# The second feed-forward stage with tokens sorted by expert into 63 tiles of 128 rows, in place of 40 dense blocks

## The reference

```python
def _L0_ffn_ref(hidden_states, gate_w, Wg, Wu, Wd, cWg, cWu, cWd):
    ...
        _, sel = jax.lax.top_k(scores, TOP_K)                 # 4 of 32
        w = jnp.take_along_axis(rw, sel, axis=-1)
        w = w / w.sum(axis=-1, keepdims=True)
    ...
    def _moe(x2d, Wg, Wu, Wd, cw):
        g = jnp.einsum('th,ehi->eti', x2d, Wg)
        u = jnp.einsum('th,ehi->eti', x2d, Wu)
        a = jax.nn.silu(g) * u * cw.T[:, :, None]
        return jnp.einsum('eti,eih->th', a, Wd)
    ...
    cw_large = jnp.zeros((T, NUM_EXPERTS), x.dtype).at[rows, sel].add(w)
    cw_small = jnp.zeros((T, NUM_CHUNK), x.dtype).at[rows, sel // GROUP].add(w)
    large = _moe(x, Wg, Wu, Wd, cw_large)
    small = _moe(x, cWg, cWu, cWd, cw_small)
    return (large + SMALL_SCALE * small).reshape(B, S, H)     # SMALL_SCALE = 0.05
```

## Time and profile before

| | before |
|---|---|
| median of 3 runs | 1463.18 us (1459.61 to 1463.65) |
| span of the profiled execution | 1454.0 us |
| median less that span | 9.2 us |
| mean granted TensorE clock | 0.802 |
| busy: PE, DVE, ACT, POOL | 86%, 78%, 55%, 38% of the span |
| first matmul of stage 1's loop, first write of stage 2's xn | 100.01 us, 430.30 us |

### The profile page before, as it was taken

The page is one execution under the profiler, slowest core; times in us unless marked ns, Lnnn a source line. Parts: engine busy times, 40 slices in busy tenths (PEclk is TensorE's granted clock), DMA queues, the critical chain, the costliest instruction groups (busy, mean ns, idle before and its releaser), DMA issues.

```text
span 1454.0 us, 30518 instructions
## 1 busy us (share of the span) xinstructions
PE 1257.3 (86%) x11458; PEld 770.0 (53%) x11458; DVE 1131.6 (78%) x2427; ACT 802.3 (55%) x1526; POOL 559.2 (38%) x619
## 2 busy tenths in 40 slices
PE   6878999999987999875899864888888989996998
PEld 3554565566553233234688742555555655563555
DVE  7858666666669999978788679898898767659785
ACT  4452444444436988873344345899899943334432
POOL 5450000000001005000333437899898938773362
PEclk9999999999996555557899985555555589997999
DMA  6111343343324999991578425998999811111010
GB/s 222 44 54 41 102 126 119 108 126 119 97 66 82 182 172 172 182 177 42 148 197 217 110 59 104 153 151 153 149 154 155 136 62 44 44 55 33 12 33 30
DMA packets 356784, 161.06 MB, mean 111 GB/s; under 512 B 330112, under 2 KB 332800, under 8 KB 356272
## 3 DMA queue, kind: packets, MB, share of 16 engines
q1 hardware_dynamic: 353344, 151.96, 48.8%
q0 software_dynamic: 1728, 4.72, 1.3%
q10 hardware_dynamic: 1584, 2.68, 0.6%
HBM read 76.79 MB, written 2.29 MB: 54 GB/s over the span
## 4 chain that ended last, share of the span: by engine, by line
PE 47%; DVE 29%; POOL 9%; ACT 5%; DMA 4%; issue 4%; SPq 1%; ACTq 0%; POOLq 0%; DVEq 0%
PE s_all L922 32%; DVE small L2397 8%; PE bank L922 6%; POOL c_hi L831 3%; POOL c_lo L831 2%; PE s_all L1331 2%; POOL c_hi L829 2%; PE s_all L1141 1%; DVE small L2400 1%; DVE stats L1909 1%; PE bank L1141 1%; DVE ffbuf L2239 1%; DVE xt_lo L1930 1%; DVE x L2255 1%; DVE xn L1922 1%
## 5 line engine op out<-in xcount | busy, mean ns | idle before, releaser
L922 PE MATMUL s_all<-xt_hi,w_hi 128*128 128x512 f16 x576 | 171.8, 380 | 17.2 <-DVE ffbuf L2195 6.6
L922 PE MATMUL s_all<-xt_hi,w_lo 128*128 128x512 f16 x576 | 171.8, 380 | 0.0
L922 PE MATMUL s_all<-xt_lo,w_hi 128*128 128x512 f16 x576 | 171.8, 380 | 0.0
L1742 ACT ACTIVATE ag<-s_all,small 128x1024 int16<-128x1024 f32 x128 | 154.1, 1204 | 23.8 <-DVE small L2400 13.8
L2397 DVE TENSOR_REDUCE small<-s_all 128x1 f32<-128x1024 f32 x128 | 155.5, 1215 | 7.8 <-PE s_all L1331 7.8
L1331 PE MATMUL s_all<-ag 32*128 32x512 f16 x256 | 130.6, 612 | 13.3 <-ACT ag L1742 8.4
L745 POOL CAST ag<-region 128x512 f16<-128x512 f32 x4 | 2.4, 611 | 346.4 <-DVE region L2361 346.4
L1582 ACT ACTIVATE hid_hi<-ffbuf 128x512 f16<-128x512 f32 x80 | 50.4, 630 | 141.1 <-DVE ffbuf L2195 141.1
L1396 PE MATMUL s_all<-ag 32*128 32x256 f16 x512 | 91.0, 399 | 35.0 <-DVE small L2477 31.4
L1804 ACT ACTIVATE ag<-ffbuf,small 128x256 f32<-128x256 f32 x256 | 115.8, 507 | 0.2
L675 POOL TENSOR_TENSOR w_hi<-w_in,ws_col 128x768 f16<-128x768 f32 (+1 forms) x40 | 56.3, 1408 | 142.5 <-PE bank L922 126.4
(11 more groups left out here) (399 smaller groups left out, 3426.7 us busy)
## 6 DMA issues: line engine op xcount, KB each, us to landing
w_in<-in_w_blocks SPq DMA_DIRECT2D x76, 384.0 KB, 4.1
w_in<-in_w_experts SPq DMA_DIRECT2D x48, 320.0 KB, 4.6
sel<-token_weights SPq DMA_DIRECT2D x46, 256.0 KB, 3.8
sel<-token_weights SPq DMA_DIRECT2D x13, 384.0 KB, 3.5
region<-in_w_attn SPq DMA_DIRECT2D x4, 512.0 KB, 10.5
sel<-token_weights SPq DMA_DIRECT2D x13, 128.0 KB, 3.9
ag<-ag SPq DMA_TRANSPOSE x66, 3.4
x<-in_x_in SPq DMA_DIRECT2D x2, 512.0 KB, 4.7
```

The lines of the kernel that those rows point to most:

```text
L922: m = nc.tensor.matmul(outp, lhs, rhs, start=(first and n == 0), stop=(last and n == len(steps) - 1), skip_group_check=True)
L1742: nc.scalar.activation(p2[n % P2_BUFS], s2[n % S2_BUFS], ACT.Exp, bias=small[:, 1, s * L2_UNITS + v:s * L2_UNITS + v + 1], scale=scale_g[s ...
```

## The change

Stage 1 no longer multiplies every token by every expert. The 4096 picks (1024 tokens by 4) are ranked by expert, and each expert's picks are rounded up to whole tiles of 128 rows; there are always 63 tiles, which is enough for any choice of the tokens. Steps, by engine:

- SP loads the weights in 16 pairs of 1 MB (two large experts and their small one); three of these loads now stand ahead of the loads of stage 0's blocks 4 to 7, and behind those blocks comes one DMA that fills the 8.3 MB of `slots1` with zeros. POOL splits three pairs into high and low parts (`pairs1`, in the manner of L675 to L679), ACT and DVE the other 13 (39 units). All stay in SBUF (`arena`).
- DVE and PE compute each pick's place (`idx1`) and a table of two offsets per tile, which say where in `arena` the weights of its experts begin.
- POOL scatters the rows of xn (high and low part, 1 KB) to their places in DRAM, in 32 indirect DMAs (L817). When all have landed, SP reads one tile after another back in transposed form (L708, five buffers).
- PE runs 63 tiles: it loads the two offsets into registers, and issues 24 matmuls of 128 columns, whose weights stand at addresses computed from the registers, and 6 of 256 columns. ACT makes the silu and the high part, DVE product and low part, now on 128 x 256 numbers each, and copies the result out of PSUM; SP stores it to DRAM (`outs1`, L713).
- POOL then gathers the results of each token's picks in 32 indirect DMAs (L826), and DVE adds each, times its weight, to x. `context2` and six units of `context4` now run on PE and ACT behind the tiles.

```diff
-SELECTED = [1]
-SEL_BLOCKS = max(FFN[l][1] for l in SELECTED)
-SPREAD = SEL_BLOCKS - 4
-SPREAD_LANDED = 16 * 2 * (SPREAD // 2)
...
+TILES1 = T * TOP1 // P + E1 - 1
...
+SPLIT1_POOL = 3
+UNITS1 = 3 * (PAIRS1 - SPLIT1_POOL)
...
+XT1_BUFS = 5
+Z1_BUFS = 2 * TOP1
+Y1_BUFS = 4
...
-CTX_GAPS = {1: (0, 3), 2: (3, 6), 3: (7, 8)}
+CTX_GAPS = {3: (7, 8)}
...
+            def pair_load(c):
+                if c >= 4:
+                    sp.wait_ge(we_land[c % 4], 16 * (c // 4))
+                if c == 9:
+                    sp.wait_ge(s_setup, 1 + len(resident))
+                if c == 12:
+                    sp.wait_ge(w_split, FFN[0][1])
+                if c == 14:
+                    sp.wait_ge(blk_done, 2 * FFN[0][1])
+                sp.dma_start(staged1(c), w_pairs[c]).then_inc(we_land[c % 4], 16)
+
+            def tile_turn(n):
+                b = n % XT1_BUFS
+                if n >= XT1_BUFS:
+                    sp.wait_ge(ex_u, n - XT1_BUFS + 1)
+                sp.dma_start(xt1[b], slots1[n * P:(n + 1) * P, :], transpose=True).then_inc(land5[b], 16)
+
+            def tile_store(n):
+                b = n % Y1_BUFS
+                sp.wait_ge(ex_out, n + 1)
+                sp.dma_start(outs1[n * P:(n + 1) * P, :], y1[b]).then_inc(land4[b], 16)
...
+            for c in range(SPLIT1_POOL):
+                pair_load(c)
+            weight_blocks(1, 2)
+            sp.wait_ge(s_setup, 1)
+            sp.dma_start(slots1.rearrange("(p n) d -> p n d", p=P),
+                         zeros16[:, :].unsqueeze(1).broadcast_to([P, TILES1, 2 * D])).then_inc(s_table, 16)
+            for c in range(SPLIT1_POOL, PAIRS1):
+                pair_load(c)
+            sp.wait_ge(ex_rows, PUT1)
+            for n in range(XT1_BUFS):
+                tile_turn(n)
+            for n in range(TILES1):
+                if n + XT1_BUFS < TILES1:
+                    tile_turn(n + XT1_BUFS)
+                if n > 1:
+                    tile_store(n - 2)
+            for n in range(TILES1 - 2, TILES1):
+                tile_store(n)
...
+            def experts1():
+
+                pool.wait_ge(s_table, 16)
+                pool.wait_ge(ex_x, 1)
+                pool.wait_ge(e1_route, 3)
+                for i in range(NT):
+                    for j in range(TOP1):
+                        nc.gpsimd.indirect_dma_start(
+                            out=slots1, out_offset=bass.IndirectOffsetOnAxis(ap=idx1[:, i, j:j + 1], axis=0),
+                            in_=rows1[:, i, :], in_offset=None).then_inc(ex_rows, 16)
+                for b in range(Y1_BUFS):
+                    pool.wait_ge(land4[b], stored1(b))
+                for i in range(NT):
+                    if i > 1:
+                        pool.wait_ge(e1_add, TOP1 * (i - 1))
+                    for j in range(TOP1):
+                        nc.gpsimd.indirect_dma_start(
+                            out=z1[(i * TOP1 + j) % Z1_BUFS], out_offset=None, in_=outs1,
+                            in_offset=bass.IndirectOffsetOnAxis(ap=idx1[:, i, j:j + 1], axis=0)
+                        ).then_inc(e1_got[i % 2], 16)
...
+                pe.wait_ge(e1_route, 5)
+                pe.wait_ge(we_first, 12 * SPLIT1_POOL)
+                pe.wait_ge(we_lo, UNITS1)
+                pe.wait_ge(ex_rows, PUT1)
+                fill(10)
+
+                offs = {}
+
+                def gate_up(n):
+                    large = pe.value_load(table[0:1, 0, n:n + 1], min_val=0, max_val=(PAIRS1 - 1) * 2 * PW + 2 * LW)
+                    small_ = pe.value_load(table[0:1, 1, n:n + 1], min_val=0, max_val=(PAIRS1 - 1) * 2 * PW + 4 * LW)
+                    offs[n] = (large, small_)
+                    pe.wait_ge(land5[n % XT1_BUFS], 16 * (n // XT1_BUFS + 1))
+                    if n > 2:
+                        pe.wait_ge(ex_hid, n - 2)
+                    xt = xt1[n % XT1_BUFS]
+                    for a in range(2):
+                        for base, low, width, c in ((large, LW, INTER1, 0), (small_, SW, P, P)):
+                            outp = bank[n % 3][0:width, 2 * a * P + c:2 * a * P + c + P]
+                            for k in range(KT):
+                                o = (2 * k + a) * width
+                                hi, lo = [arena16[:, bass.ds(base + (o + q), width)] for q in (0, low)]
+                                nc.tensor.matmul(outp, hi, xt[:, k, :], start=(k == 0), stop=False, skip_group_check=True)
+                                nc.tensor.matmul(outp, hi, xt[:, KT + k, :], start=False, stop=False, skip_group_check=True)
+                                m = nc.tensor.matmul(outp, lo, xt[:, k, :], start=False, stop=(k == KT - 1),
+                                                     skip_group_check=True)
+                    m.then_inc(ex_u, 1)
+
+                def down(n):
+                    large, small_ = offs.pop(n)
+                    pe.wait_ge(ex_hl, n + 1)
+                    if n > 3:
+                        pe.wait_ge(ex_out, n - 3)
+                    outp = bank[3 + n % 4][:, 0:D]
+                    hh, hl = hid1_hi[n % 2], hid1_lo[n % 2]
+                    for base, low, rows_, c, d0, first in ((large, LW, INTER1, 0, 4 * INTER1, True),
+                                                           (small_, SW, P, P, 4 * P, False)):
+                        hi, lo = [arena16[0:rows_, bass.ds(base + (d0 + q), D)] for q in (0, low)]
+                        nc.tensor.matmul(outp, hh[0:rows_, c:c + P], hi, start=first, stop=False, skip_group_check=True)
+                        nc.tensor.matmul(outp, hl[0:rows_, c:c + P], hi, start=False, stop=False, skip_group_check=True)
+                        m = nc.tensor.matmul(outp, hh[0:rows_, c:c + P], lo, start=False, stop=not first,
+                                             skip_group_check=True)
+                    m.then_inc(ex_y, 1)
+
+                for n in range(TILES1):
+                    gate_up(n)
+                    if n > 1:
+                        down(n - 2)
+                for n in range(TILES1 - 2, TILES1):
+                    down(n)
+                pe.wait_ge(ex_out, TILES1)
+                context2()
+                context4(0, 6)
...
+                for n in range(UNITS1):
+                    u = 3 * SPLIT1_POOL + n
+                    c = u // 3
+                    if u % 3 == 0:
+                        act.wait_ge(we_land[c % 4], 16 * (c // 4 + 1))
+                    if n > 1:
+                        act.wait_ge(we_lo, n - 1)
+                    for w, hi, _, scale in unit1(u):
+                        m = nc.scalar.activation(hi, w, ACT.Copy, scale=scale)
+                    m.then_inc(we_hi, 1)
...
+                weights_low(UNITS1)
+
+                def product(n):
+                    dve.wait_ge(ex_silu, n + 1)
+                    if n > 1:
+                        dve.wait_ge(ex_hh, n - 1)
+                    nc.vector.scalar_tensor_tensor(out=hid1[n % 2], in0=bank[n % 3][:, 2 * P:4 * P], scalar=XW * HS,
+                                                   in1=silu1[n % 2], op0=ALU.mult, op1=ALU.mult).then_inc(ex_hid, 1)
+
+                def hidden_low(n):
+                    dve.wait_ge(ex_hh, n + 1)
+                    if n > 1:
+                        dve.wait_ge(ex_y, n - 1)
+                    nc.vector.tensor_tensor(hid1_lo[n % 2], hid1[n % 2], hid1_hi[n % 2], ALU.subtract).then_inc(ex_hl, 1)
+
+                def evict(n):
+                    dve.wait_ge(ex_y, n + 1)
+                    if n >= Y1_BUFS:
+                        dve.wait_ge(land4[n % Y1_BUFS], 16 * (n // Y1_BUFS))
+                    nc.vector.tensor_copy(y1[n % Y1_BUFS], bank[3 + n % 4][:, 0:D]
+                                          ).then_inc(ex_out, 1)
+
+                for n in range(TILES1):
+                    product(n)
+                    hidden_low(n)
+                    if n > 2:
+                        evict(n - 3)
+                for n in range(TILES1 - 3, TILES1):
+                    evict(n)
+                for i in range(NT):
+                    dve.wait_ge(e1_got[i % 2], 16 * TOP1 * (i // 2 + 1))
+                    for j in range(TOP1):
+                        m = i * TOP1 + j
+                        if j:
+                            dve.wait_ge(e1_add, m)
+                        nc.vector.scalar_tensor_tensor(out=x[:, i, :], in0=z1[m % Z1_BUFS], scalar=w1[:, i, j:j + 1],
+                                                       in1=x[:, i, :], op0=ALU.mult, op1=ALU.add).then_inc(e1_add, 1)
+                    dve.wait_ge(e1_add, i * TOP1 + TOP1)
+                    measure(2, i, i + 1)
+                    context2(i)
```

More of the change, by code:

```diff
@@ L200, in build @@
         scratch = sb("scratch", [P, 3])
-        weights = sb("weights", [P, NT, 64])
-        wsplit = sb("wsplit", [P, NT, 3 * 64], F16)
+        weights = sb("weights", [P, NT, 32])
+        wsplit = part("wsplit").bitcast(F16).rearrange("p (t e) -> p t e", t=NT)
```

(55 more changed lines are left out.)

620 lines of the change are left out of this document (288 added, 332 removed).

## The result

The changed kernel takes 1503.3 us (median of 4 runs, 1497.24 to 1508.09), the kernel before 1461.74 beside it: ratio 1.0283, 95% interval 1.0255 to 1.0312, so 2.8% slower. The forecast was 1496 us. The profiled execution has a span of 1495.4 us at a mean clock of 0.776, and its own time is 1497.24 us: 1.8 us lie around the span, and the rest of the way to the median is that this execution was the fastest of the four. The table of before and the prediction put all of their 9.2 us down to what lies around the span. In the runs of the kernel before that have a span on record it is 1.8 to 2.1 us shorter than the time; the rest of the 9.2 us is that the profiled execution, with its 1454.0 us, was shorter than any of them.

A forecast was written before the change was run, and what follows sets the result against it. PE bounds stage 1, and its sequencer was to set 4.0 us a tile; xn at 211 + 63P = 463 against 430.3, +33 us on the 1454.0 span, with 9.2 around it: 1496 us. Range 1382 to 1560.

The forecast's parts named there:

- The deciding step: Tile loop: PE's register instructions, matmul issue and loads take 4.0 us a tile, with the array's 1.99 running beneath.
- P: Time of one tile in stage 1's loop: taken as 4.0 us, break-even with the kernel before at 3.48.
- Matmul issue: PE's tile loop: issuing 30 matmuls at 0.027 us each, the floor, 0.8 us a tile.
- these add: PE's tile loop: register instructions and matmuls share one instruction stream, so 2.3 + 0.8 + 0.9 = 4.0 us a tile.
- The loads: PE's tile loop: two TENSOR_LOADs at 0.45 us each, 0.9 a tile (0.2 to 2.2).
- some three register instructions: Kernel before, stage 1: what a dense block's 48 matmuls need, where a tile has 24 and 2 TENSOR_LOADs.
- Ahead of the tiles: Pair loads, routing, scatters and weight splits before the loop: first tile at 155 us, not at 100.
- covered by the scatters: Ahead of the tiles: DVE's weight splits end at 144 us, before the scatters have landed at 150.
- Behind the tiles: Last tile 5 us, 32 gathers 45, final additions and norm 6: xn starts 56 us after the tiles.
- The array sets the pace: Rival for the tile loop: P 2.0 to 2.4 us, time 1370 to 1395 us; chance 0.2.
- In between: Rival for the tile loop: registers 0.05 to 0.07, loads near 0.2, P 2.4 to 3.4, 1395 to 1458 us; chance 0.18.
- The clock falls: Rival for the tile loop: half-idle PE granted half clock, P 3.9 or 4.5, 1490 to 1527 us; chance 0.12.

The follow-up runs named there:

- e1: The changed kernel with tile weights at addresses fixed at build, so no TENSOR_LOAD or register instruction in the tile loop: 1374.73 us, ratio 0.9394 to the kernel before.
- e2: The changed kernel with the two offsets loaded once and all addresses held in registers, every tile using the first tile's weights: 1369.3 us, ratio 0.9372 to the kernel before.
- e3: The changed kernel with each tile loading its two offsets twice, 2 TENSOR_LOADs and 4 register instructions more: 1582.39 us, ratio 1.0814 to the kernel before.
- e5: The changed kernel with 8 more address register instructions a tile in gate_up, array work unchanged: 1568.75 us, ratio 1.0725 to the kernel before.
- e8: The changed kernel without gate_up's eight matmuls of high weights by low tokens, register instructions kept: 1504.5 us, ratio 1.0277 to the kernel before.
- e4: The changed kernel with POOL splitting two pairs of weights in place of three, the third going to ACT and DVE: 1494.66 us, ratio 1.0215 to the kernel before.
- e7: The changed kernel with only two of each token's four picks scattered, 16 indirect DMAs in place of 32: 1487.24 us, ratio 1.0176 to the kernel before.
- b3: b2 with `down` reordered, both products of the tile's first 128 rows, then both of the second: 1444.69 us, ratio 0.987 to the kernel before.
- b1: The changed kernel with 47 tiles of 256 rows in place of 63 of 128: 1450.47 us, ratio 0.9913 to the kernel before.
- b2: b1 with POOL splitting two pairs of weights, as in e4: 1444.87 us, ratio 0.9863 to the kernel before.

## Why the prediction was right

**The loop.** The array's work came out near the forecast: e1 takes 2.08 us a tile where the prediction had 1.99, in 63 tiles 131 us, so by the array alone the loop loses 181 us, not 187. The deciding step was that register instructions and loads on PE's own stream add up to more than the array's work. e1 and e2 show it from one side (2.1 us a tile without them, in place of 4.15), e3 and e5 from the other (more of them, tiles of 5.44 and 5.20 us by the sequencer's rows, against 4.17), e8 from the third (eight matmuls fewer, 4.15), and the sequencer's rows leave no wait for another engine in the tile. P was 4.154, forecast 4.0. Of the 7.5 us by which xn came after the forecast 463 (470.54), the loop gave 8.2, the start 2.7, and the tail gave back 3.4.

**Its terms** were sized less well than their sum, and that the sum came so close is in part luck. Of the 24 register instructions, taken at 0.095, the 20 that make addresses cost 0.13 each and the four with the loads 0.21 and 0.08: 3.2 us, where the sum had 2.3. Matmul issue was taken at 0.8 us a tile. In e8 the eight matmuls without a register instruction of their own cost nothing (4.15 us a tile against 4.17); for the others no run shows an issue apart from the 0.13. So the step that failed is the addition of the two streams, "these add", for the matmuls. The loads were taken at 0.9 for two and take 0.78: 0.30 us each (303 ns in the median of the 63 at L1170), and 0.39 to the start of the next row. The semaphore waits, 0.21, were not in the sum at all. The errors are +0.9, -0.8, -0.1 and +0.2 us: the two large ones cancel.

The trace of before has rows of PE's sequencer too. They show the "some three register instructions" of a dense block: between 156.0 and 163.8 us there are three ALU_OP rows (157.22, 161.11, 161.21). They also hold a nearer price: 32 register instructions stand directly ahead of another (L1022 ahead of L1024), 0.10 us from start to start in the mean, where the prediction went to DVE. With that, 24 of them would have come to 2.5 us in place of 2.3.

**Ahead of the tiles.** First tile at 157.68, forecast 155. The start of the scatters was off by 6.6 us (108.65, forecast 102), and another engine set it: the forecast had DVE's places last, POOL set it, with DVE's places ready at 98.7. I had left out the maximum over partitions that POOL does between `pairs1` and the scatters, with 5.6 us of idle time ahead of it, and POOL's three pairs took 46.7 us (55.83 to 102.5), not 43. e4 shows that this was the path. The trace of before has the same piece with its idle time, between the splits of the earlier trace rows:

```profile
62.07 0.39 POOL L912 PARTITION_ALL_REDUCE cmax<-cmax  x1 [6.28 <-issue]
```

Against that, the scatters took 43.0 us to the start of the last where I had 45 in all, and landing, fill and transposes 6.0 (151.69 to 157.68) where I had 8. Stage 0 lost nothing: block 4's split began at 30.25, before the 32.00 of the earlier trace rows, and the last one ended as before (55.8). The zero fill was hidden, as said: it landed 31.5 us after its issue at 23.6. That splits were "covered by the scatters" held with 14 us to spare, by e7.

**Behind the tiles.** 56 forecast. From the last tile's end, 413.76 + 4.15 = 417.9, to xn are 52.6; the gathers took 1.30 us each, not 1.4, which is the difference.

**The rivals.** "The array sets the pace" fell with the change's own loop, where PE is busy in 73% and its idle time goes to "issue" (66.8 us); e1 gives that rival's time only once the sequencer's work is gone. "In between" had a slip: registers at 0.05 to 0.07 and loads near 0.2 add up, by the prediction's own terms, to at most 2.9 us a tile, not 3.4. "The clock falls" did happen in e3, e5 and e8 (means of 0.53 to 0.79 over stretches of 40 or 50 us of their tile loops, 1.00 in the change), but in e8 it cost nothing: it has the change's time at 0.57.

## What to carry to other kernels

Sorting work by expert saves columns, but each tile here pays for its addresses on the stream that issues the matmuls: 4.17 us of sequencer rows against the 2.08 of e1. Count loads and register instructions for a tile, and compare them, at the prices measured here (some 0.65 us for a load with its two register instructions, 0.13 for an address, 0.106 for a separate semaphore wait), with the array's microseconds before choosing the tile's size. Where that stream is the longer one, try larger tiles, even if padding grows: 47 tiles of 256 rows are half as many rows again as 63 of 128, and take 50 us less (b3 against e4). Against dense work with PE busy in all 250 of 250 us, 2.5 times less array work (125 us by the prediction's estimate, against 312) did not win by itself.

## What the runs showed of the hardware that I had not expected

- A matmul that shares its address with the one before cost PE's stream nothing beside register instructions here: two matmuls and two such instructions take 0.26 us (e8), three matmuls and two 0.25 (the change).
- The granted clock differs between loops that differ little: the change holds 1.00 with PE busy in 73% of the loop; with a third fewer matmuls in gate_up (e8) it is 0.57 from 200 to 300 us, and with 1.27 us more of sequencer work a tile (e3) 0.65 to 0.79 over stretches of 40 or 50 us. What sets it no run shows. The longest idle time of the array in e8's loop was 1.21 us, in the change 1.26.
- The order of `down`'s matmuls into one bank of PSUM decides the result: with the halves' sums interleaved (b1, b2) it is 0.967 off the reference in relative error, with the halves one after another (b3) it is the reference's, at 1444.87 (b2) and 1444.69 us (b3). What happens in the bank no run looked at.
- Ahead of POOL's maximum over partitions stands an idle time of 5.6 us (5.56 in the change, 5.58 in e4 18 us earlier, 6.28 in before). In the trace it begins with two MODIFY_POOL_CONFIG rows of the same source line (102.4 in the change, 84.5 in e4, 55.7 in before), right behind the last arithmetic, so it moves with it.
